# Layer 0's scatter sums in two PSUM halves, W1 stacked twice, and VectorE's comparison row in SBUF

## What is computed

```python
# layer 0
ea = edge_attr @ W_edge.T + b_edge
msg = jax.nn.relu(x[src] + ea)
agg = jax.ops.segment_sum(msg, dst, num_segments=x.shape[0])
h = (1.0 + GIN_EPS) * x + agg
h = h @ W1.T + b1                 # then batch norm, relu, @ W2.T + b2
# layer 1
Y = jax.nn.relu(concatenate([H[src], Xe]) @ M_W.T + M_b)
Z = jax.ops.segment_sum(Y, dst, num_segments=H.shape[0])
H_next = jax.nn.relu(concatenate([H, Z]) @ U_W.T + U_b)
# around them: h = relu(layernorm(x)); x = x + layer(h)
```

## Time and profile before

| | |
|---|---|
| median of 3 runs | 4224.73 us (4224.08 to 4226.16) |
| span of the profiled execution, first to last instruction | 2879.7 us |
| PE, weight load busy | 70%, 64% of the span |
| POOL busy | 73% |
| VectorE, ScalarE busy | 53%, 33% |
| mean granted TensorE clock | 0.824 |

### The profile page before, as it was taken

How to read it: one execution, slowest core, us unless ns; L and a number is a source line. 1 busy time by engine, 2 the same in 40 slices (tenths; PEclk the granted TensorE clock), 3 DMA queues, 4 the chain that set the end, 5 groups by cost and what they waited for, 6 DMA issues and landing times.

```text
span 2879.7 us, 74534 instructions
## 1 busy us (share of the span) xinstructions
PE 2027.5 (70%) x25733; PEld 1830.1 (64%) x25733; DVE 1529.9 (53%) x2605; ACT 958.6 (33%) x2153; POOL 2097.2 (73%) x2185
## 2 busy tenths in 40 slices
PE   4678777677775777767676676766768776778772
PEld 4567666666665766657565576656647666667662
DVE  6655445344443445444454444534568776777671
ACT  2433333333332333323333233333353332323230
POOL 5777777777777777777777777777537777777774
PEclk9987887878878888788888888887869888888885
DMA  8877766777668766677667776675639998989861
GB/s 269 237 194 214 219 198 174 195 219 207 196 174 207 227 194 190 183 212 224 191 182 190 219 210 197 175 198 133 150 110 266 233 211 215 220 213 225 208 160 46
DMA packets 707917, 567.80 MB, mean 197 GB/s; under 512 B 495308, under 2 KB 609216, under 8 KB 703224
## 3 DMA queue, kind: packets, MB, share of 16 engines
q1 hardware_dynamic: 628632, 403.50, 55.1%
q0 software_dynamic: 69440, 107.94, 12.5%
q10 hardware_dynamic: 9632, 53.14, 5.3%
HBM read 296.20 MB, written 268.18 MB: 196 GB/s over the span
## 4 chain that ended last, share of the span: by engine, by line
POOL 30%; PE 24%; DMA 16%; issue 14%; SPq 7%; DVE 5%; ACT 3%; POOLq 1%; DVEq 0%; ACTq 0%
POOL edge_store L753 15%; POOL gathered_rows L783 15%; PE ps_w L1228 10%; DMA src_store<-arena 8%; PE ps_p L1163 6%; SPq L564 5%; PE ps_r L1216 4%; DMA side<-attr 4%; DMA edge_store<-side,slot_idx 2%; ACT arena L926 1%; DMA gathered_rows<-node_table_l,plain_slot 1%; PE ps_b L1198 1%; SPq L491 1%; DMA arena<-edge_store 1%; DVE ranking L1524 1%
## 5 line engine op out<-in xcount | busy, mean ns | idle before, releaser
L783 POOL DMA_INDIRECT gathered_rows<-node_table_l,plain_slot x1116 | 1066.1, 955 | 359.3 <-issue 327.2
L753 POOL DMA_INDIRECT edge_store<-side,slot_idx x1054 | 1023.3, 971 | 344.8 <-issue 325.0
L1228 PE MATMUL ps_w<-arena 128*64 128x128 f32 (+1 forms) x9040 | 922.0, 293 | 204.5 <-ACT window L934 195.7
L1228 PEld LDWEIGHTS ps_w<-arena 128*64 128x64 f32 x9040 | 787.0, 158 | 264.7 <-ACT window L934 147.3
L939 ACT ACTIVATE arena<-arena 128x512 f32<-128x512 f32 (+1 forms) x616 | 366.3, 595 | 1533.1 <-PE ps_w L1228 925.9
L1163 PE MATMUL ps_p<-w_both,side 80*128 80x128 f32 x3228 | 519.6, 317 | 425.2 <-DMA side<-attr 344.1
L1163 PEld LDWEIGHTS ps_p<-w_both,side 80*128 80x128 f32 x3228 | 461.5, 223 | 446.4 <-issue 404.0
L1630 DVE TENSOR_TENSOR arena<-ps_c,dst_rel 128x1024 f32<-128x1024 f32 (+1 forms) x476 | 525.9, 1105 | 336.1 <-PE ps_w L1228 332.7
L1615 DVE TENSOR_SCALAR arena<-arena,iota_p 125x512 bf16<-125x512 bf16 (+1 forms) x442 | 155.9, 370 | 604.5 <-DMA src_store<-arena 371.6
L1216 PE MATMUL ps_r<-tab,arena 125*128 125x64 bf16 x5100 | 245.9, 202 | 102.5 <-DVE arena L1615 60.8
L1639 DVE TENSOR_TENSOR arena<-ps_r,arena 128x512 f32<-128x512 f32 (+1 forms) x476 | 297.6, 625 | 20.3 <-PE ps_r L1216 13.4
(11 more groups left out here) (124 smaller groups left out, 1057.4 us busy)
## 6 DMA issues: line engine op xcount, KB each, us to landing
edge_store<-zeros SPq DMA_DIRECT2D x34, 3300.0 KB
arena<-edge_store SPq DMA_DIRECT2D x34, 1650.0 KB, 10.7
src_store<-arena SPq DMA_DIRECT2D x204, 256.0 KB
side<-attr SPq DMA_DIRECT2D x172, 256.0 KB
arena<-edge_store SPq DMA_DIRECT2D x34, 1056.0 KB
arena<-edge_store SPq DMA_DIRECT2D x34, 594.0 KB
plain_store<-plain_e SPq DMA_DIRECT2D x35, 512.0 KB
side<-plain_store SPq DMA_DIRECT2D x35, 512.0 KB
```

The source lines that it names most:

```text
L753: pool.indirect_dma_start(out=store, in_=stage[:, c, i, :], in_offset=None, out_offset=bass.IndirectOffsetOnAxis(ap=slot_idx[:, s, t + i:t ...
L783: pool.indirect_dma_start(out=rows[s][:, i, :], out_offset=None, in_=table[layer], in_offset=bass.IndirectOffsetOnAxis(ap=plain_slot[:, s, ...
L1228: mm = pe.matmul(ps_sum[layer][t % 2][:, 0:width], msg[:, slot, t, :], dst_match[:, slot, t, 0:width], start=(first and t <= layer), stop= ...
```

## The change

Three things are edited.

1. Layer 0 uses the scheme of layer 1: its tiles add alternately to the two halves of `ps_w`, the window copy takes all 128 partitions, and the weighting multiplies by `w1_both`, W1 stacked twice, 128 rows deep. The product of layer 0 goes to `ps_c` in place of the upper half of `ps_w`.
2. `w1_both` is loaded by two more DMAs from ScalarE's queue, and TensorE waits for them before its first matmul.
3. `iota` is now the row in the parameter tile `par` in SBUF; its copy to PSUM goes. The second copy of the columns (`col_ps`) lies in SBUF too, in `col_copies`.

```diff
+        w1_both = sb("w1_both", [P, D])
...
+        col_copies = sb("col_copies", [P, 64])
...
-        iota = ps_c[:, 0:WINDOW]
-        ps_sum = [[ps_w[0:D, 0:WINDOW]] * 2, [ps_w[i * D:(i + 1) * D, 0:WINDOW] for i in range(2)]]
-        ps_sums = [ps_w[0:D, 0:WINDOW], ps_w[:, 0:WINDOW]]
-        ps_post = [ps_w[D:2 * D, 0:WINDOW], ps_b[0][0:D, 0:WINDOW]]
-        sum_rows = [D, P]
-        col_ps = [ps_c[:, WINDOW + s * 32:WINDOW + (s + 1) * 32] for s in range(2)]
+        ps_sum = [ps_w[i * D:(i + 1) * D, 0:WINDOW] for i in range(2)]
+        ps_sums = ps_w[:, 0:WINDOW]
+        ps_post = [ps_c[0:D, 0:WINDOW], ps_b[0][0:D, 0:WINDOW]]
+        col_ps = [col_copies[:, s * 32:(s + 1) * 32] for s in range(2)]
...
+        iota = prm("iota")
...
             for i in range(2):
                 act.dma_start(u_both[i * D:(i + 1) * D, :], params[0:D, PARAMS["u_sum"]]).then_inc(w_landed, 16)
+                act.dma_start(w1_both[i * D:(i + 1) * D, :], params[0:D, PARAMS["w1_twice"]][:, 0:D]).then_inc(w_landed, 16)
...
-                act.activation(window[0:sum_rows[layer], slot, 0:width], ps_sums[layer][:, 0:width], ACT.Copy).then_inc(d.window_copied, 1)
+                act.activation(window[:, slot, 0:width], ps_sums[:, 0:width], ACT.Copy).then_inc(d.window_copied, 1)
...
-                    mm = pe.matmul(ps_sum[layer][t % 2][:, 0:width], msg[:, slot, t, :], dst_match[:, slot, t, 0:width],
-                                   start=(first and t <= layer), stop=(last and t >= nt - 1 - layer))
+                    mm = pe.matmul(ps_sum[t % 2][:, 0:width], msg[:, slot, t, :], dst_match[:, slot, t, 0:width],
+                                   start=(first and t <= 1), stop=(last and t >= nt - 2))
...
-                pe.matmul(ps_post[layer][:, 0:width], (prm("w1_twice", D)[:, 0:D], u_both[:, :])[layer], window[0:sum_rows[layer], slot, 0:width],
+                pe.matmul(ps_post[layer][:, 0:width], (w1_both, u_both)[layer][:, :], window[:, slot, 0:width],
...
-            pe.wait_ge(consts_set, 6)
-            pe.wait_ge(w_landed, 64)
+            pe.wait_ge(consts_set, 5)
+            pe.wait_ge(w_landed, 96)
...
-            dve.memset(ps_c[:, WINDOW:WINDOW + 64], -1.0).then_inc(counted_set, 1)
+            dve.memset(col_copies[:, :], -1.0).then_inc(counted_set, 1)
             dve.wait_ge(par_landed, 16)
-            dve.tensor_copy(iota, prm("iota")).then_inc(consts_set, 1)
...
-            dve.wait_ge(consts_set, 5)
+            dve.wait_ge(consts_set, 4)
```

## The result

The changed kernel took 4037.61 us (median of 4 runs, 4034.75 to 4046.82) against 4224.4 us for the kernel before on the same chip: a ratio of 0.9565, with 0.953 to 0.9601 as its 95% interval. The prediction was 4507 us, slower. It was wrong in sign.

A forecast was written before the change was run, and what follows sets the result against it. POOL's back-to-back indirect DMA orders were taken as the bound: 284 us of holds less 2 us on a 2879.7 us span gave 3162 us, plus 1345 us carried over made 4507 us. Range: 4380 to 4620 us.

The forecast's parts named there:

- I carry these 1345 us over unchanged: Whole kernel: the timed median's 1345 us above the profiled span, unexplained by any view, added unchanged to the predicted 3162 us.
- What bounds the kernel now: Opening step: in both layers' long stretches POOL issues indirect DMA orders back to back, about 1.27 us each, with no slack.
- its last rival: TensorE sets the pace in the timed runs: layer 0's 277 us of TensorE work come off, about 3950 us; chance 0.03.
- The holds: POOL orders starting during VectorE comparisons with two SBUF operands wait: 147 us in layer 0, 137 in layer 1, together 284.
- + 282 us: Sum on the 2879.7 us span: 284 us of holds less 2 us from the alternating scatter, giving 3162 us.
- Layer 0's formula for random phases: Layer 0: starts each 1.25 us fall randomly on comparisons of length d; mean hold (d - 0.12)^2 / (2 x 1.25).
- 0.64 for the five others: Layer 1, each turn: the first long comparison holds POOL 0.484 us, the five others 0.64 us each.
- The lock: Layer 1: a held order makes the next comparison hold the next one, so POOL issues one order a 1.89 us step.
- The columns: Small comparisons with the column copies, moved to SBUF: holds of 0.05 us a turn together.
- the column match: Layer 0: at 1.762 us longer than POOL's period, so each one catches a start and holds it 1.02 us.
- The alternating scatter: Layer 0: scatter matmuls fall from 150 to 68 ns, 277 us less TensorE work, but only 2 us gained.
- Weighting, window copy, start: 128 rows in place of 64, and two more loads at the start: costed at zero, 1 or 2 us if loads landed late.

The follow-up runs named there:

- e11: Kernel before, a spare comparison reading the row in SBUF ahead of each of the 616 comparisons with the row: 4241.22 us, ratio 1.0043.
- e16: The whole changed kernel, unedited, run at the 2880 us rate against the kernel before: 3097.53 us, ratio 1.0767.
- e15: Kernel before with the row read in SBUF by layer 1's comparisons alone, at the 2880 us rate: 2968.03 us, ratio 1.0299.
- e13: Kernel before with the column copies alone moved to SBUF, row still in PSUM, at the 2880 us rate: 2882.59 us, ratio 1.0002.
- e1: Kernel before, unedited, profiled again at the 4230 us rate: 4233.12 us, span 4231.3 us.
- e3: Kernel before with layer 0's scatters alternating, row and columns kept in PSUM, layer 0's product with W1 left out: 4190.87 us, ratio 0.9913.
- e18: Repeat of e3 against the kernel before, at the 4230 us rate: 4151.95 us, ratio 0.9928.
- e2: Kernel before with row and column copies moved to SBUF, layer 0's scatters as before, at the 4230 us rate: 4128.81 us, ratio 0.9774.
- e8: Kernel before with a semaphore wait and a small clearing ahead of each POOL order in the two loops: 4305.05 us, ratio 1.0214.
- e10: Kernel before, a spare comparison reading the row in PSUM ahead of each of the 616 comparisons with the row: 4332.97 us, ratio 1.0268.
- e5: Kernel before with empty instructions meant ahead of POOL's orders; the trace shows none added, so it repeats that kernel: 4230.39 us, ratio 0.9998.
- e9: Kernel before with empty instructions meant ahead of the gather matmuls; the trace shows none added, so it repeats that kernel: 4221.41 us, ratio 1.0027.
- e4: The whole changed kernel, unedited, run again at the 4230 us rate against the kernel before: 4044.99 us, ratio 0.9574.
- e17: Repeat of e2 against the kernel before, at the 4230 us rate: 4092.2 us, ratio 0.9786.
- e12: Kernel before, a spare operation with one SBUF operand ahead of each of the 616 comparisons, at the 2880 us rate: 2942.27 us, ratio 1.0218.
- run 1209: Not a run label: "the same run" is e12, and 1209 is the time in ns of a comparison in it.

## Why the prediction was wrong, point by point

**The step that failed** is the last of the sum, "I carry these 1345 us over unchanged", and with it "What bounds the kernel now": that POOL issues without a pause held for an execution of 2880 us, and the kernel is timed at 4230. At that rate POOL is idle for half of the span and TensorE is late, so that most of a delay of POOL is hidden: e11 has 174 us more of holds and spare comparisons besides, and is 12 us slower, where e16 pays its 220 us in full. The 1345 us were no overhead around the same execution but 1.5 times more time for the same matmuls. The prediction named this as its last rival (TensorE sets the pace in the timed runs, from 1.39 times slower against POOL) and gave it 0.03, because "nothing in the profile shows that". The profile didn't; but a median half as long again as the span was a sign that another execution was timed than was read, and it got no weight. The direction of that rival was right.

**The holds: the mechanism right, the size 30% too large.** At the rate that the sum was made for, its + 282 us came out as + 219.6 us: slower, as said. The view of POOL's lines in e16 splits them:

```profile
L783 POOL DMA_INDIRECT gathered_rows<-node_table_l,plain_slot x1116: 940/944/2413, 144.6 to 3062.8; - x186
```
```profile
L753 POOL DMA_INDIRECT edge_store<-side,slot_idx x1054: 954/958/3767, 22.0 to 2111.0; - x176
```

The last fetch starts 215.3 us later than in the earlier trace rows. In e15, where layer 0 is that of before, it starts 86.4 us later (2933.9 us). So layer 1 has 86 us by its time and 90 by the durations of its fetches, where 137 were forecast, and layer 0 about 129, where 147 were. Layer 0's formula for random phases was 14% high. In layer 1 the term "0.64 for the five others" was mis-sized. The lock exists: in e16's layer 1, 204 orders start inside the 204 long comparisons, as many as forecast. But they are held for 0.47 us in the mean, where (0.484 + 5 x 0.64) / 6 = 0.61 was forecast; the phase falls later in the comparison than the two steps of the earlier trace rows had it.

**The columns** were costed at 0.05 us a turn and the column match at 1.02. e13 moves the former alone and reads 1.0002. Right.

**The alternating scatter** was put at no gain at this rate beyond 2 us. Since the holds alone make up e16's whole difference, that stands. What it saves TensorE was put too high: in the stretch of 166 to 2069 us of e16 a scatter matmul takes 302.0 / 3032 = 100 ns, not 68 or 70, and TensorE is busy for 1965.5 us in all, 62 us less than before and not 280, with the clock lower. At the 4230 rate the alternation alone gains 0.8%, 29 and 37 us, of a saving that is much larger. In the stretch 200 to 2000 us of e1, and then of e3:

```profile
L1228 PE MATMUL ps_w<-arena 128*64 128x128 f32 x2081 | 393.3, 348 | 103.1 <-issue 102.3
```
```profile
L1231 PE MATMUL ps_w<-arena 128*64 128x128 f32 x2116 | 279.9, 391 | 97.5 <-issue 95.3 <-ACT arena L942 1.1
```

Busy and idle before together, 239 ns a matmul become 178, 205 us over 3400. Its neighbours give most of that back. Projection and gather in the same stretch, of e1 and then of e3:

```profile
L1163 PE MATMUL ps_p<-w_both,side 80*128 80x128 f32 x1880 | 403.3, 370 | 159.9 <-issue 105.4 <-DVE ranking L1556 36.7 <-ACT plain_e L906 16.4
...
L1216 PE MATMUL ps_r<-tab,arena 125*128 125x64 bf16 x3054 | 207.3, 216 | 202.3 <-issue 174.3 <-DVE arena L1615 27.5
```
```profile
L1166 PE MATMUL ps_p<-w_both,side 80*128 80x128 f32 x1920 | 449.6, 399 | 141.5 <-issue 60.4 <-DVE ranking L1562 42.7 <-ACT plain_e L907 36.4
...
L1219 PE MATMUL ps_r<-tab,arena 125*128 125x64 bf16 x3160 | 240.0, 229 | 271.5 <-issue 216.6 <-DVE arena L1621 54.3
```

Counted alike, a projection matmul takes 563.2 / 1880 = 300 ns, then 308, and a gather matmul 409.6 / 3054 = 134 ns, then 162. Over 3228 and 5100 of them that is 27 + 141 = 168 of the 205 us. In e18 the scatter saves 140 us by the same count, and projection and gather give back 123 + 26, so the split between the two isn't firm and the giving back is. The rival's 3950 us, all 277 us off the time, was too hopeful for that reason.

**Weighting, window copy, start**: at zero. e16's sum leaves no room for a cost of more than a few us. Right, as far as a sum can show it.

**What stays open.** Why the move to SBUF gains 91 to 96 us alone at the 4230 rate. VectorE's comparisons are no shorter (1107 ns in e2 against 1106 in e1 in the mean). H, the holds as the cause, is spoken against by e8 alone, and e8 adds work to POOL besides; Q, VectorE's reading of PSUM, fits e2, e10 and e11, but so does H where e10 and e11 are concerned. Neither is shown. The traces show where TensorE differs. While a comparison of layer 1 runs, its weight loads follow each other at a median of 53 ns in the five kernels e1, e3, e5, e9 and e18, with the row in PSUM and one comparison a step, and at 29 or 30 ns in the changed kernel, e2, e4 and e17, with the row in SBUF: 10.9 to 11.2 loads a us against 14.1 to 15.1. In layer 0 the median is 53 ns in all of them. More of these loads then fall where the higher clock is granted, and e11's spare comparisons, with the row in SBUF too, have 53 ns, so this is a difference in what meets what and no proof of a cause. The scatter and the projection show it too: together they keep TensorE busy for 1192.2 + 683.9 us in e1 and for 1193.6 + 684.5 in e9, the same program, but for 1140.9 + 621.4 in e2 and 1137.4 + 639.2 in e17.

Also open are what makes TensorE halt and what decides the rate. POOL's pauses and more traffic left the halting at 1283 and 1146 us, fewer matmuls brought it to 699, and nothing turned it off. The rate doesn't go with the chip: e1 to e4 and e12 to e15 are recorded under the same chip number, the first at 4230 and the others at 2880. Each time all runs taken together had one rate, but for two executions of the kernel before, of 5945 and 7793 us beside seventeen near 4230, which are left out of the ratios.

## What to carry to other kernels

Compare the profiled span with the timed median before reading anything else. Where they differ by more than a few per cent, the profile may be of another regime: take one that agrees, or give both regimes real chances, for the same edit can be 4% faster in one and 8% slower in the other. Cost an edit in each regime by what has slack there: a hold of POOL is paid in full where its orders follow each other with 0.30 us between them, and is mostly hidden where it waits for TensorE. Test the halves of a change together as well as apart, since here they don't add up. And look into the trace for an added instruction before a run with it is taken as evidence.

## What the runs showed of the hardware

- The same program on one core ran at 2880 or at 4230 us; VectorE, ScalarE, POOL and the largest DMA queue took equal time in both and only TensorE's matmuls were spaced out, in steps near 0.71 and 1.43 us. The mean granted clock was lower too, 0.696 against 0.824, a mix of the levels 2.4 and 1.2 GHz in both, and the spacing appeared at either level.
- A VectorE comparison with two SBUF operands holds an indirect DMA order of POOL that starts inside it, to its end. VectorE isn't held in turn by an order already begun: the comparisons' mean is 1107 ns in e2 and 1106 in e1. The Trainium skill (SBUF — State Buffer, Who interferes with whom) infers that `tensor_tensor` leaves descriptor generation alone; e15 and e16 measure the opposite, 90.5 and 219.8 us.
- One operand can hold as well. e12's spare operation, a `tensor_scalar` over 1024 numbers from SBUF in 0.773 us, raised POOL's means to 978 and 1000 ns, 25.7 + 30.6 = 56 us of holds, and the kernel became 61 us slower; I had expected no hold of it. The same section of the Trainium skill says that `tensor_scalar` can enter a mode that uses both ports and then blocks GpSimd. The holds agree with that, but no run shows the mode: 448 numbers more take the spare operation 773 - 488 = 285 ns, and a comparison of the same run 1209 - 746 = 463.
- With layer 0's scatters alternating the granted clock of 166 to 2069 us fell from 0.82 to 0.70 in e16, though TensorE was busy for less of the stretch (1222.63 against 1368.63 us), and in 200 to 2000 us the projection's matmul rose from 158 (447.3 us over 2833) to 188 ns (501.4 over 2667). At the 4230 rate the clock of that stretch is 0.67 in e1, 0.68 in e2 with the move alone, and 0.59 in e3 with the alternation alone. The stretch of e16:

```profile
166.00:2069.00 1903.00, 1222.63 (x13930) 1107.70 (x13928) 814.72 (x1509) 603.13 (x1420) 1472.86 (x1411) 0.70 0.68 188
```
